# A two-layer graph kernel: score columns split in PSUM, W·a made by TensorE in the set-up, and all engines' orders set anew

## The reference

```python
h = relu(layernorm(x))
# layer 0: graph attention, 4 heads, then one output head
Wh = einsum('bnf,hfo->bhno', h, W_heads)
f1 = einsum('bhno,ho->bhn', Wh, a_heads[:, :256]); f2 = einsum('bhno,ho->bhn', Wh, a_heads[:, 256:])
e  = leaky_relu(f1[:, :, :, None] + f2[:, :, None, :], 0.01), -1e9 where adj == 0
g  = elu(einsum('bhnm,bhmo->bhno', softmax(e), Wh))      # heads side by side: 1024 features
out = elu(the same attention on g with W_out (1024 x 256), a_out)
y  = layernorm(relu(out @ w1 + b1) @ w2 + b2 + out) * gamma + beta
x  = x + y
# layer 1
h  = relu(layernorm(x))
mi = h @ Wi.T; mj = h @ Wj.T                              # W split in halves
x  = x + deg * (mi + b) + adj @ mj
```

## Time and profile before

| | |
|---|---|
| median of 3 runs | 908.99 us (908.4 to 910.26) |
| the profiled execution | 909.05 us |
| its span, first to last instruction | 907.2 us |
| mean granted clock of TensorE | 0.989 |
| busy: PE, DVE, POOL, ACT | 836.8, 757.1, 703.9, 683.0 us |

### The profile page before, as it was taken

The page is one execution under the profiler, slowest core; times in us unless marked ns, Lnnn a source line. Parts: engine busy times, 40 slices in busy tenths (PEclk is TensorE's granted clock), DMA queues, the critical chain, the costliest instruction groups (busy, mean ns, idle before and its releaser), DMA issues.

```text
span 907.2 us, 20067 instructions
## 1 busy us (share of the span) xinstructions
PE 836.8 (92%) x6281; PEld 776.6 (86%) x6281; DVE 757.1 (83%) x1998; ACT 683.0 (75%) x1801; POOL 703.9 (78%) x948
## 2 busy tenths in 40 slices
PE   2699999999999999999999999999999999999964
PEld 1589989889998988999898899889889998989952
DVE  4978888898888889888888988888899888897753
ACT  3788878787777878778787877778777877877541
POOL 3587988877788887778888777888877788888852
PEclk9999999999999999999999999999999999999987
DMA  8100010111111011111101111110111111000000
GB/s 246 59 1 24 25 36 2 36 36 36 35 37 35 1 36 36 36 36 36 34 4 36 36 36 36 36 35 3 35 37 36 36 37 35 2 24 25 25 24 23
DMA packets 30136, 31.50 MB, mean 35 GB/s; under 512 B 1856, under 2 KB 28992, under 8 KB 30032
## 3 DMA queue, kind: packets, MB, share of 16 engines
q1 hardware_dynamic: 29776, 29.63, 10.5%
q0 software_dynamic: 256, 0.59, 0.3%
HBM read 21.82 MB, written 8.39 MB: 33 GB/s over the span
## 4 chain that ended last, share of the span: by engine, by line
PE 66%; DVE 17%; issue 9%; POOL 3%; ACT 2%; DMA 1%; SPq 0%; DVEq 0%; POOLq 0%; ACTq 0%
PE ps L1201 59%; DVE g_parts L598 4%; PE ps L1319 3%; DVE wo L711 2%; DVE lend L737 2%; PE ps L1275 2%; PE ps L1393 2%; DVE mj_lo L768 1%; DMA lend<-in_L_gnn_a_heads 1%; ACT mj_hi L1086 1%; DVE c_st L568 1%; DVE g_rest L589 1%; DVE g_parts L621 1%; DVE f_rep L669 1%; PE ps L1341 1%
## 5 line engine op out<-in xcount | busy, mean ns | idle before, releaser
L363 POOL TENSOR_TENSOR h_lo<-h2v,h_hi 128x512 fp32r<-128x512 f32 x128 | 166.6, 1302 | 0.1
L1201 PE MATMUL ps<-gh_hi,wh_hi 128*128 128x256 f32 x512 | 153.7, 300 | 1.6 <-DVE h2v L641 1.1
L1201 PE MATMUL ps<-wo_hi,h_hi 128*128 128x258 f32 x512 | 150.6, 294 | 0.0
L1201 PE MATMUL ps<-wo_lo,h_hi 128*128 128x258 f32 x512 | 145.1, 283 | 0.0
L1201 PE MATMUL ps<-wo_hi,h_lo 128*128 128x258 f32 x512 | 145.0, 283 | 0.0
L1201 PE MATMUL ps<-gh_lo,wh_hi 128*128 128x256 f32 x512 | 142.9, 279 | 0.0
L1201 PE MATMUL ps<-gh_hi,wh_lo 128*128 128x256 f32 x512 | 142.7, 279 | 0.0
L369 POOL TENSOR_SCALAR h2e<-h2e 128x512 f32<-128x512 f32 x128 | 86.2, 681 | 32.0 <-ACT h2e L959 31.8
L1201 PEld LDWEIGHTS ps<-wo_lo,h_hi 128*128 128x128 f32 x512 | 97.4, 190 | 4.3
L1201 PEld LDWEIGHTS ps<-wo_hi,h_hi 128*128 128x128 f32 x512 | 96.8, 189 | 4.6 <-POOL h_lo L363 0.4
L970 ACT ACTIVATE lend<-lend,zm 128x128 f32<-128x128 f32 x256 | 99.1, 393 | 0.0
(11 more groups left out here) (166 smaller groups left out, 2794.3 us busy)
## 6 DMA issues: line engine op xcount, KB each, us to landing
xa<-in_x SPq DMA_DIRECT2D x32, 256.0 KB, 3.1
xr<-in_x SPq DMA_DIRECT2D x32, 256.0 KB, 3.0
out<-res SPq DMA_DIRECT2D x32, 256.0 KB, 2.2
lend<-in_L_gnn_W_heads SPq DMA_DIRECT2D x4, 256.0 KB, 5.7
lend<-in_L_gnn_a_heads SPq DMA_DIRECT2D x4, 256.0 KB, 8.4
wo<-in_L_gnn_W_out SPq DMA_DIRECT2D x1, 1024.0 KB, 11.2
l1w_sb<-in_L_gnn_W SPq DMA_DIRECT2D x1, 512.0 KB, 9.7
lend<-in_L_gnn_w SPq DMA_DIRECT2D x2, 256.0 KB, 3.0
```

What stands on the lines that cost most here:

```text
L363: pool.tensor_tensor(h2_lo[:, u, :, :].rearrange("p c n -> p (c n)"), h2v[u % 2][:, :], h2_hi[:, u, :, :].rearrange("p c n -> p (c n)").bi ...
L1201: return pe.matmul(out_, lhs, rhs, start=start, stop=stop)
```

## The change

1. The score columns are split into three bf16 parts while they are columns, in PSUM (`split_cols`: 16 columns for the heads, 4 for the output head), and one bf16 matmul with a bf16 identity gives all 48 rows at once (`score_rows`, `score_rows2`). One copy then brings them to SBUF (`rows_copy` on ScalarE, `rows2_copy` on VectorE). `f_rep`, `f_rest`, `g_rest` and the 128-partition `rowsel` go; `f_cols`, `f_split`, `g_cols`, `g_split` come.
2. In the set-up TensorE makes W·a: `a` comes as 16 rows of 128, is transposed, each head's W is transposed (4 per head), and 4 products per head go into a bank of PSUM.
3. The constant rows are asked for on SP's queue behind `w_out` and `a_out`, and no longer at the start on GpSimd's.
4. The orders of `one` on all five engines are new, and so are PSUM banks (`B_HT` and the others) and the bank waits that follow from them.

```diff
+            def split_cols(name, p, cols, whole, parts):
+
+                dve.tensor_copy(whole, cols).then_inc(S[name[0]], 1)
+                dve.tensor_copy(parts[0], cols).then_inc(S[name[1] + "_first"], 1)
+                wait(dve, name[0], p)
+                wait(dve, name[1] + "_first", p)
+                dve.tensor_tensor(cols, cols, parts[0], ALU.subtract).then_inc(S[name[1] + "_rest"], 1)
+                wait(dve, name[1] + "_rest", p)
+                dve.tensor_copy(parts[1], cols).then_inc(S[name[1] + "_second"], 1)
+                wait(dve, name[1] + "_second", p)
+                dve.tensor_tensor(parts[2], cols, parts[1], ALU.subtract).then_inc(S[name[1] + "_third"], 1)
...
+                split_cols(("cols_copied", "rows"), p, ps[:, B_COLS, 0:COLS], f_cols[p.e][:, :],
+                           [f_split[p.e][:, k, :] for k in range(3)])
...
+            def wh2_scores(p):
+
+                wait(dve, "wh2_copied", p)
+                wait(dve, "rows2_done", p, lag=1)
+                split_cols(("wh2_scores_copied", "rows2"), p, ps[:, B_WH2[0]:B_WH2[0] + 2, F:WO], g_cols[p.e][:, :, :],
+                           [g_split[p.e][:, k, 0:4].rearrange("p (b j) -> p b j", b=2) for k in range(3)])
...
-                pe.transpose(ps[:, B_ROWS2, 0:P], f2_rep[p.e][:, :], ident[:, :]).then_inc(S["rows2_done"], 1)
+                wait(pe, "rows2_third", p)
+                wait_bank(p, ("rows_copied", 1, -3), ("scores_masked", 2, -2), ("probs2_copied", 1, 1), ("y_ready", 1, 2))
+                mm(ps[0:ROWS, B_ROWS2, 0:P], g_split[p.e][:, :, :].rearrange("p k r -> p (k r)"), ident_bf[:, :], True, True).then_inc(S["rows2_done"], 1)
...
-                wait(pe, "rows2_third", p)
-                wait_bank(p, ("hidden_full", 2, 1), ("mj_lo", 2, 3), ("at_lo", 2, -1))
+                wait(pe, "rows2_copied", p)
+                wait_bank(p, ("rows2_copied", 1, 0))
...
             def load_heads():
+                sp.dma_start(a_rows[:, :], a_heads.rearrange("h (r o) -> (h r) o", o=P)).then_inc(a_in, 16)
                 for hd in range(H):
                     sp.dma_start(wh[:, :, hd, :], w_heads[hd].rearrange("(c f) o -> f c o", f=P)).then_inc(heads_in[hd], 16)
-                    sp.dma_start(ah_bc[:, hd, :], a_heads[hd].partition_broadcast(P)).then_inc(heads_in[hd], 16)
...
+                for dst, src in ((beta_bc, beta), (b2_bc, b2), (gamma_bc, gamma), (l1b_bc, l1b)):
+                    sp.dma_start(dst[:, :], src.partition_broadcast(P)).then_inc(const_rows_in, 16)
                 sp.dma_start(l1w_sb[:, :, :], l1w.rearrange("(k o) d -> o k d", o=P)).then_inc(last_in, 16)
...
+            def heads_products(hd):
+
+                pe.wait_ge(wh_t_copied, hd + 1)
+                pe.wait_ge(a_cols_ready, 1)
+                for c in range(C):
+                    for k in range(C):
+                        last = mm(ps[:, B_WA, 0:COLS].rearrange("p (c j h) -> p c j h", c=C, j=2)[:, c, :, hd],
+                                  wh_t[:, hd % 2, k * F + c * P:k * F + (c + 1) * P], a_cols[:, hd, :, k], k == 0, k == C - 1)
+                last.then_inc(wa_done, 1)
```

More of the change, by code:

```diff
@@ new lines, in one @@
+                if p := pairs[5]:
+                    wh2_part(p, 1, 2)
+                    wh2_part(p, 1, 3)
+                if p := pairs[4]:
+                    h2_unit(p, 2, 0)
+                if p := pairs[6]:
+                    hidden(p, 0)
+                if p := pairs[2]:
+                    scores(p, 0)
+                if p := pairs[6]:
+                    hidden(p, 1)
+                if p := pairs[4]:
+                    h2_unit(p, 2, 1)
+                if (p := pairs[0]) and p.is_first():
+                    a_transpose()
@@ new lines, in one @@
+                if (p := pairs[0]) and p.is_first():
+                    heads_transposes(0)
+                if p := pairs[3]:
+                    prob_transposes(p, 0)
+                if p := pairs[5]:
+                    score_rows2(p)
+                if p := pairs[4]:
+                    h2_unit(p, 3, 0)
+                if (p := pairs[0]) and p.is_first():
+                    heads_transposes(1)
+                if p := pairs[5]:
+                    scores2(p)
+                if p := pairs[4]:
+                    h2_unit(p, 3, 1)
@@ new lines, in one @@
+                if (p := pairs[0]) and p.is_first():
+                    heads_transposes(2)
+                if p := pairs[4]:
+                    wh2_part(p, 0, 0)
+                    wh2_part(p, 1, 0)
+                if p := pairs[3]:
+                    prob_transposes(p, 1)
+                if p := pairs[7]:
+                    h3_transposes(p)
+                if p := pairs[3]:
+                    gh_unit(p, 0)
+                if p := pairs[6]:
+                    ffn_out(p)
+                    ffn(p, 0)
@@ new lines, in one @@
+                if (p := pairs[0]) and p.is_first():
+                    heads_products(0)
+                if p := pairs[4]:
+                    wh2_part(p, 0, 1)
+                if p := pairs[6]:
+                    ffn(p, 1)
+                if p := pairs[3]:
+                    gh_unit(p, 1)
+                if p := pairs[4]:
+                    wh2_part(p, 1, 1)
+                if p := pairs[7]:
+                    mixed(p, 0)
+                if p := pairs[5]:
+                    prob_transposes2(p)
@@ L1424, in one @@
+                if (p := pairs[2]) and p.is_first():
+                    l1w_transposes()
+                if p := pairs[1]:
+                    score_cols(p)
+                if (p := pairs[0]) and p.is_first():
+                    heads_transposes(3)
+                if p := pairs[7]:
+                    gather(p)
+                if (p := pairs[0]) and p.is_first():
+                    heads_products(2)
                 if p := pairs[4]:
-                    prob_transposes2(p)
+                    wh2_part(p, 0, 2)
```

681 lines of the change are left out of this document (308 added, 373 removed).

## The result

| | before | after |
|---|---|---|
| median, measured together (4 runs each) | 909.62 us | 920.85 us (920.3 to 921.86) |
| ratio, 95% interval | | 1.0125 (1.0108 to 1.0143) |
| span of the profiled execution | 907.2 us | 918.8 us |
| first gather, last gather of the span | 129.6, 903.2 us | 130.6, 914.7 us |
| one middle step (the median) | 26.45 us | 26.69 us |

The account below looks back on a forecast made before the run. TensorE, with a repeated wait ahead of scores2, was taken as the bound: 909.05 − 29.6 (wait) + 5.8 (new waits) − 3.2 (row matmuls) − 2.0 (set-up) = 880 us; forecast 872 to 888 (chance 0.58), wider range 869 to 896.

Parts of the forecast that it names:

- What bounds the kernel now: Steady step: TensorE waits 1.02 us ahead of scores2, 29 times; 29.6 us to gain, step 26.45 to 25.43.
- The two row matmuls: score_rows and score_rows2 on TensorE: 48 bf16 columns save 0.1 us per step, 3.2 in all; bounds 0 to 7.
- The split: VectorE's score split: ten small PSUM operations replace 4.1 us per step; busy time falls to about 21.2, no time by itself.
- The new orders: Engine orders in a step: TensorE's work sums to 25.4 us; new waits 0.2 per step (0 to 0.58), 5.8 given back.
- five thin rooms: Places in a step with little slack, such as scores2's copy (0.05 to 0.2 us) and the elu groups (0.4 to 0.9).
- `residual2`: VectorE operation reading two SBUF tiles: beside GpSimd work it can lose 0 to 1.08 us, room takes 0.5.
- the `elu`: VectorE's elu groups must end before TensorE's h2_unit and gh_unit; spare 0.4 to 0.9 us, so no wait must come.
- The set-up: Start of the kernel: W·a on TensorE and later constant rows gain 2 us; bounds 5 gained, 3 lost.
- The end: From 860 us, the last two pairs' chain has the same links less about 0.5 us: nothing taken, bounds ±3.
- Rival 2: Slower: GpSimd's ov_low waits for out_elu and ov_high, at 4 us late 1.7 per step, 924 us; chance 0.06.
- Rival 1: The wait moves on through the thin places, 0.6 us per step and more: 892 to 900 us; chance 0.25.
- The step stays above 26 us: Middle step, named sign of being wrong; the forecast was a step of 25.3 to 25.8 us.

Follow-up runs that it names:

- run 5: A kernel of TensorE matmuls alone, blocks of ten full ones plus small ones: block 1.313 us with a full small one, 1.547 with narrow weights.
- run 7: Changed kernel with all tiles padded to 128, plus add_b2 ahead of soft2 (898.53 us), x load first on SP's queue (891.62), or both (886.66).
- run 8: Changed kernel with its narrow tiles kept, plus x load first on SP's queue and add_b2 ahead of soft2: 920.95 us, ratio 1.0136.
- padded kernel: The changed kernel with its 48-row and 48-column operands filled with zeros to 128, order unchanged: 896.02 us, ratio 0.9867.
- run 1: The padded kernel: the changed kernel with all narrow operands filled with zeros to 128: 896.02 us, ratio 0.9867.
- run 2: The changed kernel with only the two row matmuls padded from 48 to 128 columns of weights: 908.83 us, ratio 1.0003.

## Why the prediction was wrong, by its steps

- **What bounds the kernel now: right.** Taking the wait at `scores2` away alone gave 22 us of the 29.6 read from it, and a median step of 25.53 where 25.43 was read.
- **The two row matmuls: here it failed.** "At least nothing is added" excluded a cost, with bounds of 0 and 0.22 us saved per step. The reason given was the size of the tile (fewer columns, bf16), and the nearest row was of a full tile. Narrow weights between full ones cost 0.234 us each time (run 5; 0.236 by runs 7 and 8), 0.47 for the two row matmuls. The six score matmuls, whose contraction fell from 128 to 48 rows, were not priced at all: another 0.70. Together 1.17 us per step, 34 us of the kernel, against 3.2 gained in the sum. Without this term the sum of the prediction would have been 883 plus what the end cost.
- **The split: right.** The ten small operations take 0.152 to 0.183 us (0.15 to 0.25 forecast), VectorE's busy time fell by 46 us in the whole span, and to 21.6 in a middle step (21.2 forecast); `yn` took a part of the gain back.
- **The new orders: right in the sum, and hidden.** TensorE's own work without the tiles is 25.5 (25.4 forecast). The 0.2 us of new waits per step (0 to 0.58) are 0.37 at the mean in the padded kernel (25.87 − 25.5), within the bounds. But of the places named (five thin rooms, `residual2`, the `elu`) none was it, since two edits elsewhere took all of it away: the waits came from `x`'s transfer behind `load_residual`, from a PSUM bank that two stages share, and from `yn`, which was 0.43 before and has a mean of 1.03 after. In the changed kernel they cost nothing, since TensorE itself is later.
- **The set-up: not gained.** The products came near the upper bound that was written down, 3.41 us for 16 and 6.8 for all (3.8 to 7.5), and the first `score_cols` 1.4 us later (the forecast reached to 1 later). The first gather is 1.0 later with about five steps of 0.24 in it, so the set-up is worth about nothing in this execution, where 2 were taken. In that of run 8, whose steps are the same, the products took 4.4 and the first gather came at 127.9 instead of 130.6, so there the forecast gain is there. The two edits of run 8 aren't the reason: with full tiles the first gather is at 127.4 without them and at 127.7 with them. The set-up gains in some executions and not in others.
- **The end: wrong, outside of its bounds.** 0 ± 3 was taken, since the chain has the same links; it costs 5.2. Which order does it stays open.
- **The rivals.** Rival 2 was on the right side with the wrong mechanism: no steady step waits for a late `ov_low`, only the emptying pipeline does, twice, for 4.2 us in all. Rival 1, the wait that moves on, is real in runs 1 and 7, at 0.37 per step and not the 0.6 it was priced at. "The step stays above 26 us" was named as the sign of being wrong, and it is what came.

The sum with the measured terms, against the step without the wait: 25.43 + 1.17 = 26.6 (26.69 measured), and over the 25 intervals between gathers in full steps (661.8 us before, 667.2 after) 5.4 us, plus 1.0 at the start and 5.2 at the end: 11.6 us.

## What to carry to other kernels

Before a matmul in a stream of full ones is made narrower (rows or columns of its weights at 64 or fewer), count how often TensorE changes between the two shapes: each time cost 0.234 us here, where the small full matmul itself cost 0.11 (1.313 less the 1.20 of ten large ones), and filling up to 128 with zeros (96 is enough by the shapes measured alone) takes it back. When the trace has no row of a new shape, the bound must reach to both sides, for every instruction whose shape changes, also those that keep their name. And before a wait is removed by a rewrite, look whether the operation that it waits for only stands beside the wrong neighbour: one moved line gave 22 of the 29 us that the whole change was to bring.

## What the runs showed of the hardware that was not expected

- The price is paid by bf16 and fp32r matmuls with few rows (fp32r with 48 rows 1.633 against 1.300) and by bf16 and fp32 with few columns (fp32 1.733 against 1.420; fp32 with few rows was not measured), but fp32r weights with 48 columns cost nothing (1.307). The Trainium skill ("PSUM — Partial Sum Buffer", section "The four PSUM rules") mentions in passing that float32r matmuls force the field for the column group to its full width; that would explain it, and the measured blocks agree.
- The same 16 small products of the set-up took 3.41 us in the changed kernel and 2.04 to 2.40 in run 2, with padded row matmuls. From 8 to 12 us the granted clock was 1.00 in both; from 12 to 16 it was 1.00 in the changed kernel and 0.58 in run 2. So a granted clock of 1.00 doesn't tell that the products run at the faster rate. The padding isn't the reason, since run 8 with narrow tiles has 2.08 and 2.35; it differs from execution to execution, and which of the two comes stays open. Products of the changed kernel, then those of the other (TensorE's timeline):

```profile
9.42 3.41 PE L1214 MATMUL ps<-a_cols,lend 128*128 128x2 f32 x16
13.58 3.41 PE L1214 MATMUL ps<-a_cols,lend 128*128 128x2 f32 x16
```

```profile
8.87 2.04 PE L1217 MATMUL ps<-a_cols,lend 128*128 128x2 f32 x16
11.24 2.40 PE L1217 MATMUL ps<-a_cols,lend 128*128 128x2 f32 x16
```
